# Edge attention on one core: scores taken four units at a time, with eight rows of relu kept instead of four

## The chip, the cores and the metric

The kernel runs on one core of one Trainium2 chip. The metric is the device time of one launch in microseconds (us), as the median of several runs. The engines are called PE (matmul), ACT (scalar), DVE (vector), POOL and SP (which issues the DMA transfers).

## The reference, cut to what matters

Four layers run over 128 graphs of 64 nodes with 256 features. The change lies in the second layer, an attention over 512 edges:

```python
x = x + _L0_gnn_ref(h, adj, ...)
h = jnp.maximum(_layernorm(x, axis=-1), 0.0)
Xq = (H @ W_lin.T).reshape(bt, n, h, dh)
Xv = (H @ W_val.T).reshape(bt, n, h, dh)
Qs = Xq[:, src]
Kt = Xq[:, dst]
e = jnp.einsum('behd,hd->beh', jax.nn.leaky_relu(Qs + Kt, LRELU_SLOPE), a)
e = e + jnp.log(A0[src, dst] + EPS)[None, :, None]
...
attn = ex / denom[src]
Y = jax.ops.segment_sum(attn[..., None] * Vt, src, num_segments=n)
return Y @ W_out.T
```

Here `e` is the score of an edge. The leaky relu is split into a linear part and a relu part; the relu part is what the text calls the scores.

## The kernel before

The second layer is the function `edge_attention`. It works in four quarters (`q` from 0 to 3) of 32 graphs. A quarter has four groups (`m`), a group has eight units (`i`), and a unit is one graph. Group 4 of a quarter (`m == NJ`) is at the same time group 0 of the next quarter. Everything is ordered by hand: each engine runs its own list of calls, and semaphores tie the lists together.

For each unit PE does `gather` (two matmuls into `c_pZ`, L1158), ACT does `relu` (two activations into one of the rows `relu_rows[i % RB]`, L1375), and PE later does `score` (L1173), which multiplies the rows of two units by a sign table into four strips of 32 partitions of `c_pE`. These matmuls have only 32 columns of weights; their form in the trace is 128\*32. The matmuls of `linear` (L1131) have the same form. All other matmuls around them have the form 128\*128.

While group `m` is scored, the rows of group `m + 1` are projected (`project`, L53 to L55, four calls in a group, after units 1, 3, 5 and 7; the text calls them projections 0 to 3), and the input of group `n = m + 2` is prepared:

- PE `turn_back` (L1109), then DVE `add_x` (L1453), `measure` (L1461) and `moments` (L1470, L1473), then POOL `normalise` (L1062, L1066, L1069) and DVE `normalise` (L1480), then PE `turn` (L1119), ACT `hi_halves`, DVE `lo_halves` (L1486), PE `linear` (L1131), ACT `copy_linear`, PE `turn_linear` (L1137), DVE `split_lin` (L1500).
- Each projection goes into the one bank `c_pU`. ACT `split_hi` (L1370) and DVE `split_lo` (L1509, L1512) empty it, and the next projection waits until `split_lo` is done.

DVE runs its own list strictly in order: `add_x`, `measure`, `split_lo` of projection 0, `moments`, `normalise`, `split_lo` of 1, `lo_halves`, `split_lo` of 2, `split_lin`, `split_lo` of 3. In group 4 the softmax over the scores is woven in (`softmax_step`, L1521 to L1527; it begins with L1521, which reads the finished `c_pE` after `add_linear`, L1179). After group 4 PE turns to the weighted sums of the quarter, beginning with `fill` (L1198). The tile `c_by_dst`, the attention matrix by destination, is written by ACT (L1418) and read by PE in that part alone. The last quarter has only groups 1 to 3, and nothing is prepared for `n` of 4 or more, so its group 2 has projections but no turns, and its group 3 has neither.

The relu rows are a ring of `RB = 4`, in the tile `c_relu`, which also serves as room for the full attention matrix after the scores. No semaphore protects the ring; the order of PE does (a `gather` stands behind the `score` that reads the row which this unit's relu will overwrite).

Of the kernel before, what the change touches and what calls it, by code (L numbers as in the profile page):

```python
# [12 lines left out]
P = 128  # L13
BATCH, NODES, D = 128, 64, 256
ROWS = BATCH * NODES
KD = D // P
# [4 lines left out]
EDGES = 512  # L21
# [46 lines left out]
def allocator(nc, ctx):  # L68
    def sb(name, shape, dt=F32):
        at = -(-nc.sbuf_base // 32) * 32  # L70
        gap = -at % LINE // 4
        if gap:
            ctx.enter_context(nc.sbuf_tensor(name + "_gap", [P, gap], F32))
        return ctx.enter_context(nc.sbuf_tensor(name, shape, dt))

    def ps(name, shape, dt=F32):
        return ctx.enter_context(nc.psum_tensor(name, shape, dt))

    return sb, ps
# [834 lines left out]
def edge_attention(core, x, x2, tables, h_rows, spilled, pairs, late):  # L914
# [4 lines left out]
    GG = GT * TILE_GRAPHS  # L919
    NJ = QT // GT  # L920
# [4 lines left out]
    with ExitStack() as ctx:  # L925
        sb, ps = allocator(nc, ctx)
        tab = tables.tab
        by_dst = sb("c_by_dst", [P, NODES, NODES])
# [6 lines left out]
        vals = sb("c_vals", [P, QT + AHEAD * GT, D])  # L935

        lin = sb("c_lin", [P, 2 * P])
        RB = 4
        dense_rows = sb("c_relu", [P, RB * KD * EDGES])
        relu_rows = [dense_rows[:, b * KD * EDGES:(b + 1) * KD * EDGES].rearrange("p (k c) -> p k c", k=KD) for b in range(RB)]  # L940

        def lin_cols(v, block):

# [46 lines left out]
        with nc.Block() as block:  # L990
# [109 lines left out]
            def _(pe):  # L1100
# [33 lines left out]
                def turn_linear(q, m):  # L1134
                    pe.wait_ge(sem["lin_row"], NJ * q + m + 1)
                    for t in range(GT):
                        last = nc.tensor.matmul(pT[:, 1, HEADS * t:HEADS * (t + 1)], lin_row[:, t * P:(t + 1) * P], tab["strip"][:, :],  # L1137
                                                start=True, stop=True)
                    last.then_inc(sem["lin_t"], 1)
# [12 lines left out]
                def gather(q, m, i):  # L1152

                    gi = QG * q + GG * m + i
                    pe.wait_ge(sem["s_lo"], QT * q + GT * m + i // 2 + 1)
                    for k in range(KD):
                        wait(pe, sem["r_done"], KD * (gi - 2) + k + 1)
                        nc.tensor.matmul(pZ[i % 2][:, k, :], keys[:, i, k * P:(k + 1) * P], tab["both"][:, :],  # L1158
                                         start=True, stop=True).then_inc(sem["z_mm"], 1)

                def score(q, m, u):

                    pair = (GG * m + 2 * u) % QG // 2
                    if pair == 0 and not m:
                        pe.wait_ge(sem["s_lo"], GT)
                    if pair == 0 and m:
                        pe.wait_ge(sem["soft"], SOFT * q + 1)
                    at = SLOTS - 2 - 2 * pair
                    for k in range(KD):
                        for i in (2 * u, 2 * u + 1):  # L1170
                            pe.wait_ge(sem["r_done"], KD * (QG * q + GG * m + i) + k + 1)
                            rows = SLOTS * (2 * (i % 2) + k)
                            nc.tensor.matmul(pE[rows:rows + SLOTS, :], tab["sign"][:, k, at:at + SLOTS],  # L1173
                                             relu_rows[i % RB][:, k, :], start=pair == 0, stop=False)

# [68 lines left out]
                def group(q, m, end=2 * NJ):  # L1244

                    n = m + 2
                    for i in range(GG):
                        gather(q, m, i)
                        if m == 0:
                            if i == 0:  # L1250
                                turn(q, 1)
                            if i == 1:
                                linear(q, 1)
                        elif n < end:
                            if i == 5:
                                turn(q, n)
                            if m == NJ and i == GG - 1:
                                turn_linear(q, n)
                                turn_attention(q)
                        if m + 1 < end and i % 2:  # L1260
                            project(q, m + 1, i // 2)
                        if i and i % 2 == 0:
                            score(q, m, i // 2 - 1)
                        elif i == 0 and m > 1:
                            score(q, m - 1, GG // 2 - 1)
                            if m == NJ:
                                add_linear(q)
                        if m == 0:
                            if i == 2:
                                turn_linear(q, 1)  # L1270
                            if i == 3:
                                turn_back(q, 2)
                            if i == GG - 1:
                                turn(q, 2)
                        elif n < end:
                            if i == 0:
                                turn_back(q, n)
                            if i == 6:
                                linear(q, n)
                            if m < NJ and i == GG - 1:  # L1280
                                turn_linear(q, n)

                def body(q, last=False):
                    top = NJ - 1 if last else NJ
                    for m in range(1, top + 1):
                        group(q, m, NJ if last else 2 * NJ)
                    score(q, top, GG // 2 - 1)
                    if last:
                        add_linear(q)
                        turn_attention(q)  # L1290
                    fill(q, 0)
                    fill(q, 1)
                    for n in range(2, NF):
                        fill(q, n)
                        turn_full(q, n - 2, last)
                    turn_full(q, NF - 2, last)
                    turn_full(q, NF - 1, last)
                    sums(q, 0)
                    for h in range(NH):
                        if h + 1 < NH:  # L1300
                            sums(q, h + 1)
                        project_out(q, h)
# [44 lines left out]
                pe.wait_ge(tables.rows, COLS_KEPT)  # L1347
                group(0, 0)
                linear(0, 2)
                score(0, 0, GG // 2 - 1)  # L1350
                turn_linear(0, 2)
                for q in range(NQ):
                    body(q, last=q == NQ - 1)

            @block.scalar
            def _(act):
# [15 lines left out]
                def relu(q, m, i):  # L1372
                    for k in range(KD):
                        act.wait_ge(sem["z_mm"], KD * (QG * q + GG * m + i) + k + 1)
                        nc.scalar.activation(relu_rows[i % RB][:, k, :], pZ[i % 2][:, k, :], ACT.Relu).then_inc(sem["r_done"], 1)  # L1375

# [69 lines left out]
            def _(dve):  # L1446
# [103 lines left out]
                def group(q, m, end=2 * NJ):  # L1550
                    n = m + 2
                    for i in range(GG):
                        if m == 0:
                            if i == 0:
                                lo_halves(q, 1)
                            if i == 2:
                                split_lin(q, 1)
                        elif n < end:
                            if i == 5:
                                lo_halves(q, n)  # L1560
                            if i == GG - 1:
                                split_lin(q, n)
                        if m == NJ and i == 0:
                            softmax_step(q, 0)
                        if m == NJ and i == GG - 1:
                            lo_of_attention(q)
                        if m and n < end and i == 3:
                            normalise(q, n)
                        if m + 1 < end and i % 2:
                            split_lo(q, m + 1, i // 2)  # L1570
                        if m == 0:
                            for at, part in ((3, add_x), (4, measure), (4, moments), (6, normalise), (7, lo_halves), (7, split_lin)):
                                if i == at:
                                    part(q, 2)
                        elif n < end:
                            for at, part in ((0, add_x), (0, measure), (1, moments)):
                                if i == at:
                                    part(q, n)
                        if m == NJ and i == 2:
                            softmax_step(q, 1)  # L1580
                        if m == NJ and i == 4:
                            softmax_step(q, 2)
                            softmax_step(q, 3)
# [926 lines left out]
```

## Time and profile before

| what | value |
|---|---|
| median of 3 runs | 2089.72 us (2087.96 to 2090.39) |
| the profiled execution, its own time | 2089.05 us |
| its span in the trace | 2087.5 us |
| PE busy | 1974.2 us, 95% of the span |
| DVE busy | 1252.9 us, 60% |
| ACT busy | 999.8 us, 48% |
| POOL busy | 223.9 us, 11% |
| edge attention in the span | from about 1143 us to about 1672 us |

The table is one execution. Times inside the span count from its start. Matmuls overlap each other, so lengths of work on PE are best read from start to start, and a busy PE is not yet a PE that never waits. A row of the timeline gives the start, the length, the engine, the line and the operation; a bracket at its end gives the idle time of the engine ahead of it and the instruction that ended it.

### The profile page before, as it was taken

What the parts mean: (1) busy time and instruction counts of PE and PEld (TensorE: products, weight loads), DVE (VectorE), ACT (ScalarE), POOL (GpSimd) and SP (SyncE); (2) the same over time, 40 slices, a digit from 0 to 9 for tenths busy, and PEclk for the clock granted to TensorE, in tenths of its full rate; (3) what the DMA queues carried; (4) which work ended last, traced back from release to release, by engine and by line L of the source; (5) the groups of instructions that cost most, each with busy time, mean ns of one, the idle gap of its engine ahead of it and who ended that gap; (6) DMA issues with size and microseconds to landing.
All of it is one profiled execution on the core that took longest, in us unless ns stands there. A gap on an engine that the chain in (4) does not pass through costs nothing. (4 is left out here: it accounts for less than half of the span.)

```text
span 2087.5 us, 33853 instructions
## 1 busy us (share of the span) xinstructions
PE 1974.2 (95%) x12438; PEld 1636.0 (78%) x12438; DVE 1252.9 (60%) x2627; ACT 999.8 (48%) x1675; POOL 223.9 (11%) x202
## 2 busy tenths in 40 slices
PE   6998999999999999999999799999999889897998
PEld 6997888888899999888887456657575778686997
DVE  7453665454455555654744666666664588886786
ACT  2553564433334433332322464563636246575996
POOL 1000000010110111011011350110100011100100
PEclk9999999999999999999999999999999989998999
DMA  3101001000100000100003221423213122001232
GB/s 117 61 21 41 0 0 41 0 0 0 40 1 0 0 0 0 31 1 41 40 0 117 95 71 51 143 81 113 98 43 125 50 80 64 22 0 51 81 101 91
DMA packets 81486, 99.92 MB, mean 48 GB/s; under 512 B 7408, under 2 KB 73584, under 8 KB 79088
## 3 DMA queue, kind: packets, MB, share of 16 engines
q1 hardware_dynamic: 81392, 98.65, 14.5%
q8 instruction: 61, 1.00, 0.2%
q14 instruction: 33, 0.27, 0.0%
HBM read 61.78 MB, written 33.55 MB: 46 GB/s over the span
## 5 line engine op out<-in xcount | busy, mean ns | idle before, releaser
L675 ACT ACTIVATE b_gate<-b_pG,b_bias 128x512 f32<-128x512 f32 (+1 forms) x504 | 304.2, 633 | 357.1 <-PE b_pG L55 356.4
L53 PE MATMUL b_pG<-b_xshi,b_whi 128*128 128x512 f32 (+1 forms) x1008 | 367.7, 365 | 6.6 <-DVE b_xslo L732 5.8
L55 PE MATMUL b_pG<-b_xshi,b_wlo 128*128 128x512 f32 (+1 forms) x1008 | 366.8, 364 | 0.0
L54 PE MATMUL b_pG<-b_xslo,b_whi 128*128 128x512 f32 (+1 forms) x1008 | 366.8, 364 | 0.0
L728 DVE CAST b_xshi<-HT 128x512 fp32r<-128x512 f32 (+3 forms) x144 | 59.6, 456 | 268.0 <-PE b_pG L55 267.7
L53 PEld LDWEIGHTS b_pG<-b_xshi,b_whi 128*128 128x128 f32 x1008 | 189.7, 188 | 33.9 <-DVE b_xslo L732 6.0
L54 PEld LDWEIGHTS b_pG<-b_xslo,b_whi 128*128 128x128 f32 x1008 | 189.8, 188 | 25.6
L55 PEld LDWEIGHTS b_pG<-b_xshi,b_wlo 128*128 128x128 f32 x1008 | 189.6, 188 | 25.8
L53 PE MATMUL b_pG<-b_hshi,b_whi 128*128 128x512 f32 (+1 forms) x576 | 205.1, 356 | 0.0
L54 PE MATMUL b_pG<-b_hslo,b_whi 128*128 128x512 f32 (+1 forms) x576 | 205.1, 356 | 0.0
L55 PE MATMUL b_pG<-b_hshi,b_wlo 128*128 128x512 f32 (+1 forms) x576 | 205.1, 356 | 0.0
L683 ACT ACTIVATE b_tc<-b_cell 128x512 f32<-128x512 f32 (+1 forms) x144 | 83.7, 581 | 213.4 <-DVE b_cell L871 111.6
L696 POOL TENSOR_TENSOR b_gate<-b_gate 128x512 f32<-128x512 f32 (+1 forms) x72 | 83.4, 1158 | 930.9 <-ACT b_gate L675 930.9
L1375 ACT ACTIVATE c_relu<-c_pZ 128x512 f32<-128x512 f32 x256 | 138.2, 596 | 35.7 <-PE c_pZ L1158 34.5
L53 PEld LDWEIGHTS b_pG<-b_hshi,b_whi 128*128 128x128 f32 x576 | 108.1, 188 | 12.5
L55 PEld LDWEIGHTS b_pG<-b_hshi,b_wlo 128*128 128x128 f32 x576 | 108.1, 188 | 12.5
L54 PEld LDWEIGHTS b_pG<-b_hslo,b_whi 128*128 128x128 f32 x576 | 108.1, 188 | 12.4
L732 DVE TENSOR_TENSOR b_xslo<-HT,b_xshi 128x512 fp32r<-128x512 f32 (+1 forms) x144 | 101.4, 746 | 2.5
L875 DVE TENSOR_TENSOR HT<-b_gate,b_tc 128x512 f32 (+3 forms) x72 | 51.9, 720 | 67.0 <-ACT b_tc L683 67.0
L1158 PE MATMUL c_pZ<-t_both,c_keys 128*128 128x512 f32 x256 | 87.8, 426 | 0.0
L1158 PEld LDWEIGHTS c_pZ<-t_both,c_keys 128*128 128x128 f32 x256 | 42.6, 191 | 45.3 <-issue 31.9
L878 DVE TENSOR_TENSOR b_tc<-b_gate,b_tc 128x512 f32<-128x512 f32 (+1 forms) x72 | 44.0, 611 | 54.7 <-ACT b_tc L683 54.7
(344 smaller groups left out, 3976.5 us busy)
## 6 DMA issues: line engine op xcount, KB each, us to landing
a_xt<-in_x SPq DMA_DIRECT2D x16, 512.0 KB, 5.5
h_scratch<-HT SPq DMA_DIRECT2D x4, 2048.0 KB, 7.6
l_x<-in_x SPq DMA_DIRECT2D x16, 512.0 KB, 3.9
l_w<-h_scratch SPq DMA_DIRECT2D x16, 512.0 KB, 5.0
x_scratch<-l_x SPq DMA_DIRECT2D x16, 512.0 KB, 3.1
c_x<-x_scratch SPq DMA_DIRECT2D x32, 256.0 KB, 3.7
x_scratch<-c_x SPq DMA_DIRECT2D x32, 256.0 KB, 2.5
l_x<-x_scratch SPq DMA_DIRECT2D x16, 512.0 KB, 3.8
```

The costliest lines, as they stand in the source:

```text
L53: nc.tensor.matmul(out, w_hi, x_hi, start=first, stop=False)
L54: nc.tensor.matmul(out, w_hi, x_lo, start=False, stop=False)
L55: return nc.tensor.matmul(out, w_lo, x_hi, start=False, stop=last)
L675: nc.scalar.activation(gate[s][:, g, 0:plan.n], pG[s][:, g, 0:plan.n], SIG[g], bias=bias[:, plan.p - 1, 2 * g + s:2 * g + s + 1])\
L683: nc.scalar.activation(tc[s][:, 0:plan.n], cell[b][:, s, 0:plan.n], ACT.Tanh).then_inc(tanh_ready, 1)
L696: nc.gpsimd.tensor_tensor(gate[s][:, I, 0:plan.n], gate[s][:, I, 0:plan.n], gate[s][:, G, 0:plan.n], ALU.mult).then_inc(ig_ready, 1)
L728: nc.vector.tensor_copy(plan.flat(xs_hi[b][:, k, :]), plan.windows(it, b, k, t))\
L732: last = nc.vector.tensor_tensor(plan.flat(xs_lo[b][:, k, :]), plan.windows(it, b, k, t), plan.flat(f32(xs_hi[b][:, k, :])), ALU.subtract)
L875: nc.vector.tensor_tensor(plan.windows(it, b, s, t), plan.flat(gate[s][:, O, :]), plan.flat(tc[s][:, :]), ALU.mult).then_inc(h_ready, 1)
L878: nc.vector.tensor_tensor(tc[s][:, 0:n], gate[s][:, O, 0:n], tc[s][:, 0:n], ALU.mult).then_inc(h_ready, 1)
L1158: nc.tensor.matmul(pZ[i % 2][:, k, :], keys[:, i, k * P:(k + 1) * P], tab["both"][:, :], start=True, stop=True).then_inc(sem["z_mm"], 1)
L1375: nc.scalar.activation(relu_rows[i % RB][:, k, :], pZ[i % 2][:, k, :], ACT.Relu).then_inc(sem["r_done"], 1)
```

## The change

The ring of relu rows grows from four to eight. The first four stay in `c_relu`, the other four lie in `c_by_dst`. `score` is called twice in a row, four units in one go: units 0 to 3 of a group after projection 2 of the same group's unit 5, and units 4 to 7 after projection 0 in the next group. The first softmax step moves from unit 0 to unit 2 of group 4, because `add_linear` moves from unit 0 to unit 1.

```diff
-        RB = 4
-        dense_rows = sb("c_relu", [P, RB * KD * EDGES])
-        relu_rows = [dense_rows[:, b * KD * EDGES:(b + 1) * KD * EDGES].rearrange("p (k c) -> p k c", k=KD) for b in range(RB)]
+        RB = GG
+        dense_rows = sb("c_relu", [P, RB // 2 * KD * EDGES])
+        halves_of_ring = (dense_rows[:, :], by_dst[:, :, :].rearrange("p i j -> p (i j)"))
+        relu_rows = [part[:, b * KD * EDGES:(b + 1) * KD * EDGES].rearrange("p (k c) -> p k c", k=KD)
+                     for part in halves_of_ring for b in range(RB // 2)]
...
-                        if i and i % 2 == 0:
-                            score(q, m, i // 2 - 1)
-                        elif i == 0 and m > 1:
-                            score(q, m - 1, GG // 2 - 1)
+                        if i == GG // 2 + 1:
+                            score(q, m, 0)
+                            score(q, m, 1)
+                        elif i == 1 and m > 1:
+                            score(q, m - 1, 2)
+                            score(q, m - 1, 3)
                             if m == NJ:
                                 add_linear(q)
...
-                    score(q, top, GG // 2 - 1)
+                    score(q, top, 2)
+                    score(q, top, 3)
...
-                score(0, 0, GG // 2 - 1)
+                score(0, 0, 2)
+                score(0, 0, 3)
...
-                        if m == NJ and i == 0:
+                        if m == NJ and i == 2:
                             softmax_step(q, 0)
```

In the changed file the lines of PE's list stand two further down (L1173 is L1175, L1131 is L1133) and those of DVE's list six further down (L1473 is L1479).

PE, a regular group, from the end of projection 2 to the gather of unit 7. `c_pU` is the bank of the projections, `c_pZ` that of the gathers, `c_pE` holds the scores, `c_pT` takes the linear part. Before:

```order
L55 MATMUL c_pU<-t_wqv_hi,c_hTlo 128x512
L1158 MATMUL c_pZ<-t_both,c_keys 128x512 x2
L1173 MATMUL c_pE<-c_relu,t_sign 32x512 x4
L1131 MATMUL c_pT<-c_hThi,t_wl 32x512 x2
L1131 MATMUL c_pT<-c_hTlo,t_wl 32x512 x2
L1158 MATMUL c_pZ<-t_both,c_keys 128x512 x2
```

The same place with the change:

```order
L55 MATMUL c_pU<-t_wqv_hi,c_hTlo 128x512
L1175 MATMUL c_pE<-c_relu,t_sign 32x512 x8
L1160 MATMUL c_pZ<-t_both,c_keys 128x512 x2
L1133 MATMUL c_pT<-c_hThi,t_wl 32x512 x2
L1133 MATMUL c_pT<-c_hTlo,t_wl 32x512 x2
L1160 MATMUL c_pZ<-t_both,c_keys 128x512 x2
```

Two scores (x8) now stand here where one (x4) did, and a gather separates them from the linear matmuls, which touched a score before. One such score less stands between projection 0 and projection 2 at each of the two places after units 2 and 4.

PE, the border between two regular groups, from turning the linear part to projection 0. Before:

```order
L1137 MATMUL c_pT<-t_strip,c_lin_row 128x4 x4
L1158 MATMUL c_pZ<-t_both,c_keys 128x512 x2
L1173 MATMUL c_pE<-c_relu,t_sign 32x512 x4
L1109 MATMUL c_pT<-t_ident,l_w_53 128x128 x8
L1158 MATMUL c_pZ<-t_both,c_keys 128x512 x2
L53 MATMUL c_pU<-t_wqv_hi,c_hThi 128x512
```

With the change:

```order
L1139 MATMUL c_pT<-t_strip,c_lin_row 128x4 x4
L1160 MATMUL c_pZ<-t_both,c_keys 128x512 x2
L1111 MATMUL c_pT<-t_ident,l_w_53 128x128 x8
L1160 MATMUL c_pZ<-t_both,c_keys 128x512 x2
L53 MATMUL c_pU<-t_wqv_hi,c_hThi 128x512
```

The score ahead of the turn back is gone from here; it follows, with another one, behind projection 0.

DVE, group 4 of the first quarter, from the end of group 3 to its normalise. `l_x_50` and `l_w_52` are the input tiles of the group being prepared. Before:

```order
L1512 TENSOR_TENSOR c_keys<-c_pU,c_keys 64x256 x2
L1521 TENSOR_TENSOR c_work<-c_pE,t_log_w 128x512
L1453 TENSOR_TENSOR l_x_50<-c_pT,l_x_50 128x1024
L1459 MEMSET c_ve 128x4
L1461 BN_STATS c_st<-l_x_50 128x6 x4
L1509 COPY c_vals<-c_pU 128x256
L1512 TENSOR_TENSOR c_keys<-c_pU,c_keys 64x256 x2
L1468 MEMSET c_unused 128x1
L1470 BN_AGGR c_mv<-c_st 128x2 x4
L1473 TENSOR_TENSOR c_ve<-c_ve,c_mv 128x4
L1523 SCALAR_TENSOR_TENSOR c_work<-t_cut,c_work 128x512
L1480 TENSOR_SCALAR l_w_52<-l_x_50,c_mv,c_rstd 128x256 x2
```

With the change:

```order
L1518 TENSOR_TENSOR c_keys<-c_pU,c_keys 64x256 x2
L1459 TENSOR_TENSOR l_x_50<-c_pT,l_x_50 128x1024
L1465 MEMSET c_ve 128x4
L1467 BN_STATS c_st<-l_x_50 128x6 x4
L1515 COPY c_vals<-c_pU 128x256
L1518 TENSOR_TENSOR c_keys<-c_pU,c_keys 64x256 x2
L1474 MEMSET c_unused 128x1
L1476 BN_AGGR c_mv<-c_st 128x2 x4
L1479 TENSOR_TENSOR c_ve<-c_ve,c_mv 128x4
L1527 TENSOR_TENSOR c_work<-c_pE,t_log_w 128x512
L1529 SCALAR_TENSOR_TENSOR c_work<-t_cut,c_work 128x512
L1486 TENSOR_SCALAR l_w_52<-l_x_50,c_mv,c_rstd 128x256 x2
```

The first softmax step (L1521, now L1527) moves from ahead of `add_x` to behind `moments`, next to the first scan (L1523, now L1529).

## Rows read from the trace of the kernel before

**Rows 1.** Windows: length, busy PE, PEld, DVE, ACT, POOL, PE clock, DMA, GB/s.

```profile
1194.00:1200.00 6.00, 3.74 (x20) 1.11 (x20) 1.43 (x2) 1.45 (x2) 6.00 (x3) 0.72 0.53 175
1346.24:1365.15 18.91, 18.23 (x108) 10.51 (x104) 11.99 (x30) 13.21 (x26) 3.09 (x3) 1.00 0.27 84
```

**Rows 2.** Timeline of PE, group 3 of the second quarter.

```profile
1365.15 1.09 PE L1109 MATMUL c_pT<-t_ident,l_w 128*128 128x128 f32 x8
...
1366.55 0.40 PE L53 MATMUL c_pU<-t_wqv_hi,c_hThi 128*128 128x512 f32 x1
...
1370.32 0.50 PE L53 MATMUL c_pU<-t_wqv_hi,c_hThi 128*128 128x512 f32 x1
...
1374.42 1.09 PE L1119 MATMUL c_pT<-t_ident,l_w 128*128 128x128 f32 x8 [0.33 <-DVE l_w L1480]
1375.74 0.50 PE L53 MATMUL c_pU<-t_wqv_hi,c_hThi 128*128 128x512 f32 x1 [0.23 <-DVE c_keys L1512]
...
1377.23 0.62 PE L1158 MATMUL c_pZ<-t_both,c_keys 128*128 128x512 f32 x2
1377.78 1.06 PE L1173 MATMUL c_pE<-c_relu,t_sign 128*32 128x512 f32 x8
1378.67 0.59 PE L1131 MATMUL c_pT<-c_hThi,t_wl 128*32 128x512 f32 x1
...
1379.64 0.74 PE L1158 MATMUL c_pZ<-t_both,c_keys 128*128 128x512 f32 x2
1380.22 0.40 PE L53 MATMUL c_pU<-t_wqv_hi,c_hThi 128*128 128x512 f32 x1
...
1381.61 0.95 PE L1137 MATMUL c_pT<-t_strip,c_lin_row 128*128 128x4 f32 x8
...
1383.07 1.06 PE L1173 MATMUL c_pE<-c_relu,t_sign 128*32 128x512 f32 x8
```

**Rows 3.** Timeline of DVE, the same group.

```profile
1366.28 1.23 DVE L1453 TENSOR_TENSOR l_x<-c_pT,l_x 128x1024 f32<-128x1024 f32 x1 [0.81 <-PE c_pT L1109]
...
1372.01 2.35 DVE L1480 TENSOR_SCALAR l_w<-l_x,c_mv,c_rstd 128x256 f32<-128x256 f32 x2 [1.12 <-POOL c_rstd L1062]
...
1382.60 0.36 DVE L1500 COPY c_lin<-c_pT 64x16 f32<-64x16 f32 x2 [3.06 <-PE c_pT L1137]
...
1383.43 0.86 DVE L1512 TENSOR_TENSOR c_keys<-c_pU,c_keys 64x256 fp32r<-64x256 f32 x2
```

**Rows 4.** Timeline of all engines, group 4 of the second quarter.

```profile
1390.62 1.22 DVE L1523 TENSOR_TENSOR_SCAN c_work<-t_cut,c_work 128x512 f32<-128x512 f32 x1
...
1390.78 1.86 POOL L1062 TENSOR_TENSOR c_rstd<-c_ve,c_mhalf 128x4 f32<-128x4 f32 x1 [16.57 <-DVE c_ve L1473]
...
1395.09 1.09 PE L1119 MATMUL c_pT<-t_ident,l_w 128*128 128x128 f32 x8 [1.18 <-DVE l_w L1480]
...
1396.41 0.50 PE L53 MATMUL c_pU<-t_wqv_hi,c_hThi 128*128 128x512 f32 x1 [0.23 <-DVE c_keys L1512]
```

**Rows 5.** Timeline of PE, end of group 4 and first matmul of `fill`.

```profile
1399.75 0.62 PE L1131 MATMUL c_pT<-c_hThi,t_wl 128*32 128x512 f32 x2 [0.23 <-DVE c_hTlo L1486]
...
1404.39 1.07 PE L1173 MATMUL c_pE<-c_relu,t_sign 128*32 128x512 f32 x8
1405.38 0.50 PE L1198 MATMUL c_pZ<-edge_pairs,c_attnhi 128*128 128x512 f32 x1
```

**Rows 6.** Timeline of the last quarter: projection 2 of group 1, then group 3.

```profile
1582.65 0.50 PE L53 MATMUL c_pU<-t_wqv_hi,c_hThi 128*128 128x512 f32 x1 [0.23 <-DVE c_keys L1512]
...
1604.53 0.61 PE L1158 MATMUL c_pZ<-t_both,c_keys 128*128 128x512 f32 x2
...
1614.54 1.08 ACT L1375 ACTIVATE c_relu<-c_pZ 128x512 f32<-128x512 f32 x2 [0.58 <-PE c_pZ L1158]
...
1616.65 1.13 PE L1179 MATMUL c_pE<-t_both,c_lin 128*128 128x512 f32 x2
```

**Rows 7.** Timeline of PE, the longest pause ahead of `linear` in the first quarter.

```profile
1196.26 1.07 PE L1131 MATMUL c_pT<-c_hThi,t_wl 128*32 128x512 f32 x2 [2.46 <-DVE c_hTlo L1486]
```

## The prediction

> **What bounds the kernel now.** I read the table of windows first [rows 1], then the timelines of PE and DVE for one regular group [rows 2, 3], then group 4 and the ends of the quarters [rows 4 to 6]. PE is busy for 18.23 of the 18.91 us of a regular group [rows 1], so the stage looks bound by PE. The rows of PE say otherwise. `turn` (L1119) waits for DVE's normalise, and projection 2 waits for DVE's `split_lo` (L1512) [rows 2]. A group is therefore a loop of two parts. From the turn back (1365.15) to projection 2 (1375.74) DVE's chain decides: 10.59 us, in which PE has slack. From projection 2 to the end of turning the linear part PE decides: it never waits, and 5.87 us pass until `turn_linear` (1375.74 to 1381.61) [rows 2]. What matters is thus in which part a score stands.
>
> DVE's chain in numbers: `add_x` starts at 1366.28, normalise at 1372.01 [rows 3], and projection 2 follows at 1375.74 [rows 2], 9.46 us after `add_x`. At the other end `split_lin` starts at 1382.60 and the last `split_lo` ends at 1383.43 + 0.86 = 1384.29 [rows 3], 2.68 us after `turn_linear`. Today the next turn back comes so late (another score is ahead of it) that `add_x` waits for it, 0.81 us in the row shown [rows 3].
>
> **The price of a score.** Two matmuls of 128\*128 form are 0.23 us apart: six take 1.39 (1380.22 to 1381.61) [rows 2]. A score that stands alone takes 0.99 us (1404.39 to 1405.38) [rows 5], one that is followed by `linear` 0.89, and `linear` behind it 0.97 [rows 2]. So joined pieces take 1.86 instead of 1.98. Two gathers take 0.46 by themselves, 0.55 ahead of a score (1377.23 to 1377.78), and 0.58 behind a burst of 32-column matmuls (1379.64 to 1380.22) [rows 2]. Each burst that vanishes thus saves 0.12 + 0.09 + 0.12 = 0.33 us of PE, and each score that stays costs 0.86 to 0.89.
>
> The change takes bursts away. By the order of PE's list a regular group had four (the last score of the group before, score 0, score 1, score 2 with `linear`) and now has three, since `linear` stands alone. Over the stage 19 vanish: four in each of three quarters, five in the last, two in the first group. That is 19 × 0.33 = 6.3 us of PE time.
>
> The Trainium skill has the rule behind this ("TensorEngine Tiling (Array Packing)", Key Properties): changing the tiling mode drains the TensorE. The trace agrees, with 0.33 us for a burst. By that rule alone, with PE as the bound, the kernel gains the 6.3 us; the rows of waits speak against it, and the case is the first rival below.
>
> **A regular group, term by term.** Projection 2 is followed by two scores: 1.49 + 0.09. The two scores take 1.86. The gather of unit 6 between two bursts takes 0.46 + 0.12 + 0.09 = 0.67. `linear` alone takes 0.99, the gather of unit 7 0.58, projection 3 1.39. Sum to `turn_linear`: 7.07 us, against 5.87. Then two routes lead to the next projection 2. Over the turn back: 1.46 less the 0.09 that a following score cost, so 1.37 (1381.61 to 1383.07) [rows 2], and the 10.59 of before: 19.03. Over DVE: 2.68 to the end of the last `split_lo`, 0.02, and 9.46 from `add_x`: 19.23. The longer decides: 19.23 against 18.91, **+0.32 us a group**. PE's part holds two scores as before, but both now stand ahead of `turn_linear`; before, one stood behind it, in the time in which DVE emptied projection 3. Leaving that space pays only until `add_x` meets the last `split_lo`. There are five such groups (the first quarter has one; between its projections 2 of groups 1 and 2 POOL's work on the edge pairs decides, so I add 0): **+1.6**.
>
> **Group 4.** From projection 2 of group 3 to that of group 4 pass 20.67 us (1375.74 [rows 2] to 1396.41 [rows 4]). With the change 7.07 + 2.70 us pass until `add_x`. From there it is the 9.46 of a regular group and what the softmax adds. Today POOL's power (L1062) starts at 1390.78 beside the scan (L1523) and takes 1.86 us [rows 4], while DVE's whole wait for it is 1.12 in a regular group [rows 3]; that adds 0.85, so 10.31. The change puts softmax step 0 between `moments` and the scan. At the least it fits in: step 0 and the scan end about when normalise starts today, −0.1. At the most the power again ends after the scan, which is now later by the length of step 0 (about 0.7): +0.6. No row shows the new pairing, so I take the middle, +0.25: 7.07 + 2.70 + 10.56 = 20.33, **−0.34**, three times: **−1.0** (bounds −2.1 and 0).
>
> The Trainium skill ("SBUF — State Buffer", SBUF: two separate sides) says that a DVE operation with two SBUF inputs and a GpSimd operation that reads SBUF exclude each other, the first to start holding the ports for its whole length. The row of 1.86 agrees. Step 0 reads one input from PSUM, so by this rule the power starts first, the scan waits for it and normalise comes 0.3 us later than today: the same as the middle.
>
> **The ends of the quarters.** From projection 2 of group 4 to `fill` pass 8.97 us (1396.41 [rows 4] to 1405.38 [rows 5]). In it stand score 2, `linear` and score 3; then four scores and `linear`. Two more scores are 1.72, one more burst 0.33. Today `linear` waits for `lo_halves` in between (0.23 us of idle PE in its row [rows 5], which I take as 0.41 with the restart, the 8.97 less the prices of its pieces); the longer way hides that. **+1.64** each, three times: **+4.9**. What follows `fill` starts from it and only shifts.
>
> **The last quarter.** From projection 2 of group 1 (1582.65) to the first gather of group 3 (1604.53) pass 21.88 us [rows 6]. Then: 7.07 to `turn_linear`, 2.73 until `split_lo` lets projection 0 go, and for group 2 1.58 + 1.86 + 0.58 + 0.46 = 4.48 (projection 0, two scores, two gathers), 3.77 (projection 0 to 1 through ACT and DVE, 1366.55 to 1370.32 [rows 2], now between projections 1 and 2), 4.48 and 1.39: 23.92, **+2.0**. Group 3 is bound by the loop of ACT and PE: ACT pauses 0.58 us ahead of every second relu [rows 6], since a gather stands behind a score that waits for a relu. With eight rows the gathers run ahead of the scores and two of four pauses go: 11.4 instead of 12.12 us (1604.53 to 1616.65) [rows 6], **−0.7** (bounds −1.4 and 0).
>
> **The start.** The first group wins 0.6 us ahead of its turn and then has one more score behind `linear`, in a stretch where the clock stands at 0.72 of full in the mean [rows 1]: 0.86 to 1.6. **+0.5**.
>
> **Costs of nothing.** Rows of relu written into `c_by_dst` instead of `c_relu` are the same activations; the tile is free then, and its next writer waits on PE work behind all scores. No DMA, no queue of SP or POOL is touched; loads are issued on `turn` and land a whole group ahead.
>
> **Sum:** 0.5 + 1.6 − 1.0 + 4.9 + 2.0 − 0.7 = +7.3 us. Against the profiled execution's own 2089.05 us that is 2096.4 us; it is 0.67 below the median of the runs, which I leave in the range.
>
> **Rivals.** (1) *PE's sum decides*, and the kernel is faster. It would be so if DVE's chain had slack. All 6.3 us would come back: 2082.8 us. The bracketed waits of L1119 and L53 [rows 2] speak against it. It decides only if the way from the turn back to projection 2 falls below PE's own sum there, about 8.9 us by the prices above, against 10.59. Chance 0.08. (2) *The overlap is better than I allow*: `add_x` follows the turn back directly (+0.1 instead of +0.32 a group, since 19.03 is the other route), the softmax fits in at its lower bound (−2.1), and group 3 saves 1.4. Sum 0.5 + 0.5 − 2.1 + 4.9 + 2.0 − 1.4 = +4.4; with the start at 0 as well it is +3.9, 2093.0 us, no change that can be told. Chance 0.2. (3) *The clock falls*. PE's pauses in the slack part grow, from 1.18 us ahead of `turn` in group 4 [rows 4] to some 1.5 us ahead of projection 1 in a group 1 (3.77 us of ACT and DVE against 2.3 of PE) and as much ahead of its `turn`. Behind a pause of 2.46 us [rows 7] the granted clock was at its lower level, 1.2 GHz, for part of the stretch, 0.72 in the mean over 6 us [rows 1], which is 1.7 us of PE lost. Two such stretches more give 2099.8 us. Chance 0.15. My forecast has the remaining 0.57.
>
> **The numbers.** A difference of 0.2%, 4.2 us, is about what a measurement of this kernel can tell from none. The forecast's own range is 2094.5 to 2098.5. The range that leaves out two in ten reaches from 2089.5, over rival 2, to 2100.0, over rival 3. Slower: 0.57 + 0.15 and a little of rival 2, 0.73. Same: 0.17. Faster: 0.10.
>
> **What the profile after would show.** Nineteen bursts less and less PE busy time, but longer idle ahead of `turn` and of projections 1 and 2. 19.2 us from turn back to turn back in a regular group; DVE without idle ahead of `add_x`; 10.6 us from projection 2 of group 4 to `fill`; L1062 in group 4 near 1.0 or near 1.9 us. The prediction fails if two scores in a row take clearly less than 1.86 us, or if projection 2 comes less than 9.4 us after `add_x`.

## The result, and the profile after

| | before | after |
|---|---|---|
| device time, median (lowest to highest) | 2089.11 us (2087.96 to 2090.39), 6 runs | 2097.19 us (2095.82 to 2101.83), 6 runs |
| ratio, 95% interval | 1 | 1.0039 (1.0027 to 1.0051) |
| profiled execution: own time, span | 2089.05, 2087.5 us | 2096.91, 2095.3 us |
| PE busy | 1974.2 us | 1966.9 us |
| first turn back of the stage to the last `fill` | 481.50 us | 490.05 us |

The change makes the kernel 8.1 us slower, though PE is busy for 7.3 us less in it (4.9 us less in a second trace of it, below). Forecast were 2096.4 us and 6.3 us less work. PE's list has 46 bursts of 32-column matmuls in the stage instead of 65: the 19 of the forecast. Line numbers move by 2 in PE's functions (turn back L1111, `turn` L1121, `linear` L1133, `turn_linear` L1139, gather L1160, score L1175, `add_linear` L1181, `fill` L1200) and by 6 or less in those of DVE and ACT (`add_x` L1459, normalise L1486, `split_lo` L1518).

The table of windows of the changed kernel, first: length, busy PE, PEld, DVE, ACT, POOL, granted clock, DMA share, GB/s. The first row is a regular group from turn back to turn back, the counterpart of the second row of [rows 1]. The other two are the same step, projection 2 to `turn_linear` of a group 1, in the last and in the second quarter.

```profile
1349.89:1369.18 19.29, 17.84 (x105) 10.64 (x105) 12.07 (x30) 13.10 (x27) 3.08 (x3) 1.00 0.25 82
1588.77:1597.38 8.61, 8.61 (x40) 4.16 (x41) 2.49 (x4) 4.25 (x8) 0.00 (x0) 0.80 0.74 263
1341.35:1348.39 7.04, 7.04 (x40) 3.53 (x41) 2.49 (x4) 4.25 (x8) 0.00 (x0) 1.00 0.49 157
```

A regular group takes 19.29 us instead of 18.91, though PE is busy for 0.39 us less of it. The second and third row do the same work at two clocks. At a mean of 0.80 of full, part of the stretch at the lower of the two levels (1.2 GHz), it takes 1.57 us more.

The timeline of PE in the changed kernel, group 3 of the second quarter, the group of [rows 2]:

```profile
1369.18 1.06 PE L1111 MATMUL c_pT<-t_ident,l_w 128*128 128x128 f32 x8
...
1372.04 1.92 PE L1175 MATMUL c_pE<-c_by_dst,t_sign 128*32 128x512 f32 x16
1373.89 1.20 PE L1160 MATMUL c_pZ<-t_both,c_keys 128*128 128x512 f32 x4
...
1378.52 1.09 PE L1121 MATMUL c_pT<-t_ident,l_w 128*128 128x128 f32 x8 [1.16 <-DVE l_w L1486]
1379.85 0.50 PE L53 MATMUL c_pU<-t_wqv_hi,c_hThi 128*128 128x512 f32 x1 [0.23 <-DVE c_keys L1518]
...
1381.45 1.92 PE L1175 MATMUL c_pE<-c_relu,t_sign 128*32 128x512 f32 x16
1383.30 0.73 PE L1160 MATMUL c_pZ<-t_both,c_keys 128*128 128x512 f32 x2
1383.96 0.62 PE L1133 MATMUL c_pT<-c_hThi,t_wl 128*32 128x512 f32 x2
...
1386.91 0.95 PE L1139 MATMUL c_pT<-t_strip,c_lin_row 128*128 128x4 f32 x8
1387.71 0.72 PE L1160 MATMUL c_pZ<-t_both,c_keys 128*128 128x512 f32 x2
1388.40 1.06 PE L1111 MATMUL c_pT<-t_ident,l_w 128*128 128x128 f32 x8
```

Each x16 row is two scores in a row. They take 1.85 us to the next row's start, less than twice the 0.99 of one that stands alone [rows 5]. The bracket of `turn` shows what became of the saving: PE waits 1.16 us for DVE's normalise, against 0.33 before [rows 2]. From projection 2 (1379.85) to `turn_linear` (1386.91) PE works without a wait, and needs 7.06 us. No score stands between `turn_linear` and the next turn back any more.

The timeline of DVE behind that `turn_linear`:

```profile
1387.89 0.36 DVE L1506 COPY c_lin<-c_pT 64x16 f32<-64x16 f32 x2 [4.23 <-PE c_pT L1139]
...
1388.72 0.86 DVE L1518 TENSOR_TENSOR c_keys<-c_pU,c_keys 64x256 fp32r<-64x256 f32 x2
1389.61 1.22 DVE L1459 TENSOR_TENSOR l_x<-c_pT,l_x 128x1024 f32<-128x1024 f32 x1
```

`split_lin` (L1506) waits for PE, for 4.23 us instead of 3.06 [rows 3]. `add_x` (L1459) has no bracket: it follows `split_lo` at once, where it had waited 0.81 us for the turn back [rows 3]. The way over DVE decides, as forecast.

Group 4 of the second quarter, all engines:

```profile
1394.24 0.69 DVE L1527 TENSOR_TENSOR c_work<-c_pE,t_log_w 128x512 f32<-128x512 f32 x1
1394.28 1.01 POOL L1064 TENSOR_TENSOR c_rstd<-c_ve,c_mhalf 128x4 f32<-128x4 f32 x1 [15.97 <-DVE c_ve L1479]
...
1394.97 1.23 DVE L1529 TENSOR_TENSOR_SCAN c_work<-t_cut,c_work 128x512 f32<-128x512 f32 x1
...
1395.37 1.66 POOL L1068 TENSOR_TENSOR l_w<-l_x,c_mv 128x512 f32<-128x512 f32 x1
...
1396.23 2.06 DVE L1486 TENSOR_SCALAR l_w<-l_x,c_mv,c_rstd 128x256 f32<-128x256 f32 x2
```

The power (L1064) starts beside softmax step 0 (L1527) and takes 1.01 us, not 1.86 as beside the scan [rows 4]. Now L1068, which starts beside the scan, is long: 1.66 us, where the operation takes 1.04 elsewhere (below).

The end of that group, PE:

```profile
1399.55 0.50 PE L53 MATMUL c_pU<-t_wqv_hi,c_hThi 128*128 128x512 f32 x1
...
1408.31 1.93 PE L1175 MATMUL c_pE<-c_by_dst,t_sign 128*32 128x512 f32 x16
1410.16 0.50 PE L1200 MATMUL c_pZ<-edge_pairs,c_attnhi 128*128 128x512 f32 x1
```

1399.55 to 1410.16 is 10.61 us, against 8.97 before.

The last quarter, PE, as in [rows 6]:

```profile
1588.77 0.50 PE L53 MATMUL c_pU<-t_wqv_hi,c_hThi 128*128 128x512 f32 x1 [0.23 <-DVE c_keys L1518]
...
1608.30 0.50 PE L53 MATMUL c_pU<-t_wqv_hi,c_hThi 128*128 128x512 f32 x1 [1.29 <-DVE c_keys L1518]
...
1614.15 1.07 PE L1160 MATMUL c_pZ<-t_both,c_keys 128*128 128x512 f32 x4
...
1625.58 0.70 PE L1181 MATMUL c_pE<-t_both,c_lin 128*128 128x512 f32 x1
```

In group 2 the two scores of group 1's second half now stand between projections 0 and 1, and PE then waits 1.29 us ahead of projection 2 for DVE (the row of 1608.30). From 1588.77 to the gathers of group 3 at 1614.15 pass 25.38 us instead of 21.88, and 11.43 instead of 12.12 from there to `add_linear`.

### The profile page after: what moved, and what is told of

The parts are those of the page before. It is cut to its first block and busy times, and to the rows that moved or that the text cites. A ratio compares the mean times of both kernels' runs of the same rounds, so it can differ in the third digit from the quotient of the medians.

```text
span 2095.3 us, 33852 instructions
## 1 busy us (share of the span) xinstructions
PE 1966.9 (94%) x12438; PEld 1639.2 (78%) x12438; DVE 1250.9 (60%) x2627; ACT 996.2 (48%) x1675; POOL 222.9 (11%) x202
## 5 line engine op out<-in xcount | busy, mean ns | idle before, releaser
L1381 ACT ACTIVATE c_relu<-c_pZ 128x512 f32<-128x512 f32 x128 | 67.6, 600 | 38.5 <-PE c_pZ L1160 38.4
L1160 PE MATMUL c_pZ<-t_both,c_keys 128*128 128x512 f32 x256 | 82.7, 426 | 0.1
L1381 ACT ACTIVATE c_by_dst<-c_pZ 128x512 f32<-128x512 f32 x128 | 67.5, 602 | 22.4 <-PE c_pZ L1160 22.0
```

## The experiments

Theory: the cost lies in where the scores stand. From projection 2 to `turn_linear` every microsecond of PE is one of the kernel's. Behind the turn back and up to projection 2, PE has slack. Rivals: the ring of eight rows, with half of it in another tile, costs something by itself; or PE's work costs the same wherever it stands; or the clock does it.

The ratios below are those on record; they are not the quotient of the two medians, and can differ from it by 0.05%.

### The ring alone

The kernel before, with the scores in their old places.

```diff
-        RB = 4
-        dense_rows = sb("c_relu", [P, RB * KD * EDGES])
+        RB = GG
+        dense_rows = sb("c_relu", [P, RB // 2 * KD * EDGES])
+        halves_of_ring = (dense_rows[:, :], by_dst[:, :, :].rearrange("p i j -> p (i j)"))
```

> The kernel before with the ring of eight relu rows (four of them in the attention matrix's room) and every score where it was. The theory that the places of the scores cost the time: no change, within 1 us of the kernel before, since no instruction moves. The rival that the rows in the attention matrix's tile or the longer ring cost something: up to the whole +8 us of the change.

Measured: 2090.03 us (10 runs) against 2089.48 (22 runs), ratio 0.9998 (0.9988 to 1.0008). A regular group takes 18.91 us and the stage 481.59, as before (481.50). The eight rows cost nothing that can be told.

### Eight spare transposes in the slack part

The kernel before, with 8 transposes (0.97 us of PE) that nothing reads, behind the gather of unit 4 in thirteen groups.

```diff
+                        if m and n < end and i == 4:
+                            spare(q, n)
```

> The kernel before with eight spare transposes of a constant on PE behind the gather of unit 4, in 13 groups, in the part between turn back and projection 2 (their result is not used). Eight transposes take 0.8 us. Theory: PE has 1.4 us of waits in that part, so no change, at most +1 us. The rival that PE's sum of work decides the time of the stage: 13 x 0.8 = +10.5 us.

Measured: 2088.93 us (10 runs) against 2089.48, ratio 0.9997 (0.9988 to 1.0007). PE in the second quarter:

```profile
1374.19 1.03 PE L1248 MATMUL c_pT<-t_ident 128*128 128x128 f32 x8
1375.16 1.06 PE L1173 MATMUL c_pE<-c_relu,t_sign 128*32 128x512 f32 x8
...
1376.72 1.04 PE L1119 MATMUL c_pT<-t_ident,l_w 128*128 128x128 f32 x8
1377.65 0.50 PE L53 MATMUL c_pU<-t_wqv_hi,c_hThi 128*128 128x512 f32 x1
```

The brackets of `turn` and of projection 2 are gone: the transposes fill both waits. The brackets understate these: from `turn` to projection 2 pass 0.93 us here and 1.32 before [rows 2]. The loop keeps its length (18.90 us). Thirteen times 0.97 us of PE's work cost nothing here.

### The same transposes ahead of the turn back

The kernel before, in the same thirteen groups.

```diff
+                    if m > 2:
+                        for t in range(GT):
+                            for k in range(KD):
+                                nc.tensor.transpose(pTr[:, t, k * P:(k + 1) * P], tab["ident"][:, :], tab["ident"][:, :])
```

> The kernel before with the same eight spare transposes in the same 13 groups, but directly ahead of the turn back, in the part in which PE does not wait. Theory: every one counts but in the one group that POOL decides: 12 x 0.8 = +9.8 us. The rival that there is slack all around the loop: clearly less, under +5 us. (The rival of PE's sum gives +10.5 us here and in the run with the transposes behind unit 4 alike.)

Measured: 2098.78 us (5 runs) against 2089.48, ratio 1.0042 (1.0028 to 1.0056). PE:

```profile
1370.73 1.09 PE L1110 MATMUL c_pT<-t_ident 128*128 128x128 f32 x8
1371.66 1.04 PE L1113 MATMUL c_pT<-t_ident,l_w 128*128 128x128 f32 x8
...
1380.87 1.09 PE L1123 MATMUL c_pT<-t_ident,l_w 128*128 128x128 f32 x8 [0.32 <-DVE l_w L1484]
1382.19 0.50 PE L53 MATMUL c_pU<-t_wqv_hi,c_hThi 128*128 128x512 f32 x1 [0.23 <-DVE c_keys L1516]
```

The waits behind stand as before, and the regular group takes 19.77 us, 0.86 more; the stage is 10.75 us longer. The work is of the same kind as in the kernel above and costs 9.3 us in all. The place decides, not PE's sum.

### `linear` alone, a score behind it

The kernel before, with score 2 behind the gather of unit 7. As many scores as before stand on either side of `turn_linear`, but `linear` is no longer joined to one, so a group has one burst more.

```diff
+                        if i == GG - 1:
+                            score(q, m, 2)
                         if m + 1 < end and i % 2:
                             project(q, m + 1, i // 2)
-                        if i and i % 2 == 0:
+                        if i in (2, 4):
                             score(q, m, i // 2 - 1)
```

> The kernel before with linear ahead of score 2: linear behind the gather of unit 6, score 2 behind that of unit 7. No work is added, one burst of 32-column matmuls more in each group, in the part in which PE does not wait. Theory (0.33 us for a burst, and linear now waits some 0.1 us for lo_halves in a regular group and longer in group 4): +0.45 us a regular group, about +1.0 us at the end of each of three quarters, together about +7 us: 2096.5 us. The rival that a burst costs nothing of its own: +0.1 us a regular group and +3 us together.

Measured: 2096.15 us (6 runs) against 2089.38 (10 runs), ratio 1.0032 (1.002 to 1.0045). PE, and DVE's `lo_halves`:

```profile
1378.70 0.50 PE L53 MATMUL c_pU<-t_wqv_hi,c_hThi 128*128 128x512 f32 x1 [0.23 <-DVE c_keys L1514]
...
1379.56 1.23 DVE L1488 SCALAR_TENSOR_TENSOR c_hTlo<-c_pT,c_hThi 128x1024 fp32r<-128x1024 f32 x1 [0.92 <-ACT c_hThi L1361]
...
1380.19 0.62 PE L1158 MATMUL c_pZ<-t_both,c_keys 128*128 128x512 f32 x2
1380.93 0.62 PE L1131 MATMUL c_pT<-c_hThi,t_wl 128*32 128x512 f32 x2
...
1381.93 0.73 PE L1158 MATMUL c_pZ<-t_both,c_keys 128*128 128x512 f32 x2
1382.59 1.07 PE L1173 MATMUL c_pE<-c_relu,t_sign 128*32 128x512 f32 x8
...
1385.09 0.95 PE L1137 MATMUL c_pT<-t_strip,c_lin_row 128*128 128x4 f32 x8
```

From projection 2 to `turn_linear` 6.39 us pass instead of 5.87, and the regular group takes 19.42 instead of 18.91: +0.52 and +0.51. What PE loses in the part where it decides, the loop loses, and 6.8 us in all. The loss is more than the 0.33 us at which I price a burst. The difference is ahead of `linear`: the gathers take 0.74 us until it starts (1380.19 to 1380.93), and took 0.55 ahead of a score [rows 2]. These 0.19 us are a wait for `lo_halves` (L1488), though it has no bracket: that ends at 1379.56 + 1.23 = 1380.79, and `linear` starts 0.14 us later. Where a bracket names this wait, `linear` follows as closely (0.15 us in the kernel before, where `lo_halves` ends at 1399.60 [rows 5]). So the 0.52 us are 0.33 for the burst, as priced, and 0.19 of wait.

### The first scan behind normalise

The kernel before. It tells whether the long power of group 4 is the scan's doing.

```diff
+                        if m == NJ and i == 3:
+                            softmax_step(q, 1)
...
-                        if m == NJ and i == 2:
-                            softmax_step(q, 1)
```

> The kernel before with the first scan of the softmax behind DVE's normalise in group 4, so that POOL's power runs with no scan beside it. Theory: the power takes 1.0 us instead of 1.86, and projection 2 of group 4 comes about 0.9 us earlier behind that of group 3 (19.8 instead of 20.67 us); lo_halves comes a scan later, so the way from there to fill gets about 1.1 us longer (10.1 instead of 8.97), and the whole is unchanged within 1 us. The rival that the power is long for another reason (its input lands late): 1.86 us again.

Measured, one run: 2092.5 us. Group 4, all engines:

```profile
1391.32 1.01 POOL L1062 TENSOR_TENSOR c_rstd<-c_ve,c_mhalf 128x4 f32<-128x4 f32 x1 [16.55 <-DVE c_ve L1473]
...
1392.37 2.35 DVE L1480 TENSOR_SCALAR l_w<-l_x,c_mv,c_rstd 128x256 f32<-128x256 f32 x2 [1.12 <-POOL c_rstd L1062]
1392.41 1.04 POOL L1066 TENSOR_TENSOR l_w<-l_x,c_mv 128x512 f32<-128x512 f32 x1
```

Without a scan beside it the power takes 1.01 us, and the way between the projections 2 of groups 3 and 4 is 19.80 us instead of 20.67. The scan then delays what comes later (projection 2 to `fill` 10.23 instead of 8.97), so the stage is 1.04 us longer. The whole time is 3.1 us above the kernel before, of one run, so 2 us of it are not the stage's.

### Both scores ahead of `turn`

The changed kernel, with scores 0 and 1 behind the gather of unit 5 and ahead of `turn`.

```diff
                         gather(q, m, i)
+                        if i == GG // 2 + 1:
+                            score(q, m, 0)
+                            score(q, m, 1)
...
-                        if i == GG // 2 + 1:
-                            score(q, m, 0)
-                            score(q, m, 1)
-                        elif i == 1 and m > 1:
+                        if i == 1 and m > 1:
```

> The changed kernel with one move: scores 0 and 1 stand right behind the gather of unit 5, ahead of the turn and of projection 2, so in the part in which PE waits for DVE. Theory of the places: from projection 2 to turn_linear 7.07 us fall to about 5.4 (then bound by the emptying of projection 2), the part before it becomes bound by PE at about 11 us, and a regular group takes about 17.6 us instead of 19.2 (18.9 before). A quarter gains about 3.7 us against the kernel before, the sum is about -9.7 us: 2079 us. The rival that pairs of scores, or the mode of 32 columns in long bursts, cost time wherever they stand: 2097 us as the change. The rival that DVE's chain cannot be shortened because the last split_lo is what ends it: no better than 2089 us.

Measured: 2083.18 us (6 runs) against 2089.48, ratio 0.9967 (0.9955 to 0.998), faster than both kernels. PE:

```profile
1359.31 0.62 PE L1133 MATMUL c_pT<-c_hThi,t_wl 128*32 128x512 f32 x2 [0.62 <-DVE c_hTlo L1492]
...
1371.96 1.93 PE L1175 MATMUL c_pE<-c_relu,t_sign 128*32 128x512 f32 x16
1373.81 1.09 PE L1121 MATMUL c_pT<-t_ident,l_w 128*128 128x128 f32 x8
1374.66 0.48 PE L53 MATMUL c_pU<-t_wqv_hi,c_hThi 128*128 128x512 f32 x1
```

The waits ahead of `turn` and projection 2 are gone, and a regular group takes 17.78 or 18.06 us. It is not the 17.6 I expected, and the kernel is 4 us slower than the 2079 expected. A new wait stands ahead of `linear`: PE arrives before DVE's `lo_halves` and loses 0.62 us. Projection 2 to `fill` takes 11.82 us in the first quarter, against 9.33 in the others. In part it is a stretch of low clock at 1278.9, which the kernel before does not have. The other part came before that stretch:

```profile
1273.40 1.28 ACT L1385 ACT_TABLE_LOAD   x1
...
1277.65 1.05 PE L1139 MATMUL c_pT<-t_strip,c_lin_row 128*128 128x4 f32 x8 [0.99 <-ACT c_lin_row L1369]
```

ACT loads a table here, 1.28 us long, ahead of its work for the first quarter's softmax; in the second quarter there is no load at this place, and no such wait. `copy_linear` is late by it, and projection 2 to `turn_linear` takes 5.57 us instead of 4.62. The 1.54 us that remain lie in the low stretch.

### One score ahead of `turn`, one behind the gather of unit 6

The changed kernel again, with one of the two scores moved behind it, to fill that new wait.

```diff
                         gather(q, m, i)
+                        if i == GG // 2 + 1:
+                            score(q, m, 0)
...
-                        if i == GG // 2 + 1:
-                            score(q, m, 0)
+                        if i == GG // 2 + 2:
                             score(q, m, 1)
-                        elif i == 1 and m > 1:
+                        if i == 1 and m > 1:
```

> The changed kernel with score 0 ahead of the turn and score 1 behind the gather of unit 6, joined to linear. As many bursts and as much work as with both ahead of the turn (2083 us, 17.8 to 18.1 us a regular group). Theory: from projection 2 to turn_linear 5.8 us, then DVE's route of 2.7 + 9.46: 17.9 us a regular group, 2083 us again, now bound by DVE on one side. The rival that only the number of scores ahead of the turn decides: half way between the change and both ahead, 2090 us.

Measured: 2081.98 us (5 runs) against 2089.38, ratio 0.9962 (0.9948 to 0.9976). PE:

```profile
1372.87 1.09 PE L1121 MATMUL c_pT<-t_ident,l_w 128*128 128x128 f32 x8 [0.15 <-DVE l_w L1487]
1374.20 0.50 PE L53 MATMUL c_pU<-t_wqv_hi,c_hThi 128*128 128x512 f32 x1 [0.23 <-DVE c_keys L1519]
```

A regular group takes 18.03 or 18.12 us. The wait ahead of `linear` is gone in the regular groups, the small ones ahead of `turn` and projection 2 are back. The kernel isn't measurably better than with both scores ahead (the intervals overlap), and it beats the kernel before by 7.4 us.

### The change once more

One more profile of the changed kernel, for the stretches of low clock.

> The changed kernel once more, for a second trace. If the clock falls behind the longer pauses of the change, its two extra stretches at the lower level (at 1312.7 and 1589.1 us) come again at the same steps of the program; if they depend on where the stage happens to start, they move, go or others come. Regular groups 19.2 to 19.3 us and group 4 19.7 us in any case.

Measured, one run: 2095.91 us. Regular groups of 19.22 and 19.29 us and a group 4 of 19.72 us repeat. The low clock does not. The first trace has two stretches that the kernel before lacks: one at 1312.7, in the part behind `fill`, and one at 1589.1, behind projection 2 of the last quarter's group 1. This one has neither. It has two others, at 1214.1 and 1463.3, both behind projection 2 of a group 1, and lacks one that the kernel before and the first trace have at 1233.4 and 1234.2. The one at 1214.1 costs nothing in all: from projection 2 of the first quarter's group 1, in which it lies, to that of group 2 pass 21.30 us, as in the other two traces, since POOL's work decides there. So this trace has one stretch that costs (1463.3) where the kernel before has one (1233.4), and their stages can be compared as they are. The window of the step with the stretch at 1463.3, in the third quarter:

```profile
1462.90:1471.50 8.60, 8.60 (x40) 4.16 (x41) 2.49 (x4) 4.24 (x8) 0.00 (x0) 0.80 0.48 160
```

The step that took 7.04 us in the second quarter of the first trace takes 8.60 here, at a clock of 0.80.

### The pauses of groups 1 filled

The changed kernel, with the 8 spare transposes behind the gathers of units 3 and 4 of each group 1, where the change leaves PE idle longest.

```diff
+                        if m == 1 and i in (3, 4):
+                            spare(q, n)
```

> The changed kernel with eight spare transposes of a constant on PE behind each of the gathers of units 3 and 4, in group 1 of each quarter alone, where the change leaves PE its longest pauses (about 1.4 us ahead of projection 1 and 1.5 us ahead of the turn). Theory: the clock falls behind these pauses in some of the groups 1; filled, they cost nothing (the part from turn back to projection 2 stays 10.5 us) and no group 1 has a stretch at the lower level: 1.5 us less for each one that goes, 2095 us in the mean. The rival that the clock falls for another reason (the phase of the stage, the DMA traffic beside group 1): stretches there again, 2097 us.

Measured: 2097.33 us (9 runs) against 2090.01 (12 runs), ratio 1.0034 (1.0024 to 1.0044). The window from turn back to projection 2 of the second quarter's group 1:

```profile
1332.94:1343.47 10.53, 9.21 (x55) 7.36 (x54) 8.39 (x21) 7.99 (x17) 3.08 (x3) 1.00 0.83 242
```

It stays 10.53 us long with the spare work in it, as expected. None of this trace's four groups 1 has a stretch of low clock; the change's two traces have one and two of four, that of before none. But the one in the part behind `fill` is there again, at 1314.9, and the time is that of the change (2095 us were expected, but the intervals are too wide to tell a stretch of 1.5 us for certain). So the pauses of groups 1 aren't shown to cause the stretches, nor cleared: the traces are too few.

## Why the prediction was right

It forecast 2096.4 us and slower, and 2097.19 was measured. By its own steps, with the same places of both traces:

| step | forecast | measured |
|---|---|---|
| start, first turn back to that of group 1 | +0.5 | +0.71 (57.51 to 58.22) |
| five regular groups | +1.6 | +1.61 |
| group 4, three times | −1.0 | −2.85 |
| projection 2 of group 4 to `fill`, three times | +4.9 | +4.90 |
| last quarter to the gathers of group 3 | +2.0 | +3.50, of it 1.54 low clock |
| its group 3 | −0.7 | −0.69 |
| low clock behind the first `fill` | 0 (rival 3) | +1.45 |
| ahead of the stage, and behind it | 0 | +0.37, −1.05 |

The rows add up to +7.95, the spans differ by 7.87. The stage alone is 8.55 longer by its two ends, and its rows add up to 8.63. The last row lies in parts that the change does not touch; it moves from trace to trace (+1.30 ahead and +0.07 behind in the second).

**The two routes.** Forecast were 7.07 us to `turn_linear` and 19.23 us a regular group over DVE. The trace has 7.06 and 19.21 to 19.29. The absent wait of `add_x` names the route. The spare transposes test the two parts of the loop: nothing in the slack part, 0.86 us a group ahead of the turn back. The way to `turn_linear` is 1.19 us longer than before, which is a second score at 0.86 and a burst at 0.33. Rival 1, that PE's sum decides, fell: PE's busy time shrank by 5 to 7 us and the kernel got slower. Bursts taken away make the kernel faster only where the scores stand in the slack part: with both ahead of `turn` it is 6.3 us faster than before, with one of them 7.4.

**The Trainium skill** says that changing the tiling mode drains the TensorE ("TensorEngine Tiling (Array Packing)", Key Properties). The trace agrees: joined, two scores take 1.85 us and not 1.98, and one burst more cost 0.33 us in its experiment, beside 0.19 us of wait. The rule says nothing of where that price is paid, and here that decides the sign.

**Group 4, the step that was mis-sized.** The mechanism was right: the group gets shorter, because step 0 moves into a gap and no score stands behind `turn_linear`. The size was −0.95 a group, not −0.34, and beyond my lower bound (−0.7). The term was `add_x` to projection 2: forecast 10.56, measured 9.94 (1389.61 to 1399.55). I had taken the middle of two pairings. It was the lower one: power beside step 0, and normalise 6.62 us behind `add_x` (1389.61 to 1396.23), as before. The bound then missed that normalise itself gets shorter, 2.06 us where it took 2.28 in this group and 2.35 in a regular one [rows 3]. That the scan is what stretches the power is shown by the kernel with the scan behind normalise: 1.01 us and −0.87 us a group.

What sets the length of normalise can be read from the traces, though no run was made for it. It has two halves on DVE, and two operations of POOL run beside them. At the start of the stage in the changed kernel POOL is ahead of DVE, and the second half has no POOL operation beside it:

```profile
1151.80 1.10 POOL L1071 TENSOR_TENSOR l_w<-l_w,c_rstd 128x512 f32<-128x512 f32 x1
1152.04 1.33 DVE L1486 TENSOR_SCALAR l_w<-l_x,c_mv,c_rstd 128x256 f32<-128x256 f32 x2
```

That half takes 0.40 us. Each half that has a POOL operation beside it ends 0.15 to 0.16 us behind that operation, in every trace of this case. Here it is the first half, at 1153.05 behind 1152.90. The median length of a half is 1.20 us. In group 4 of the changed kernel L1068 has started beside the scan and ends only 0.80 us behind the start of normalise, not 1.01 as before, so the first half is 0.95 us long and not 1.16. Of the 0.37 us between the 10.31 us of the group before and the 9.94 after, this is 0.22; 0.03 is an earlier start and 0.12 an earlier `split_lo` behind it. So POOL's share of normalise lengthens the very chain of DVE that decides in the slack part. Whether the kernel would gain by moving that share, no run tests.

The Trainium skill ("SBUF — State Buffer", SBUF: two separate sides) gives the ports to whichever of the two operations starts first, for its whole length. By this rule the scan had to wait for the power; it started at 1394.97, while the power by its row (spans on POOL are rough) ran until 1394.28 + 1.01 = 1395.29, and was 1.23 us long as ever. The other half of the rule fits: the POOL operation that starts beside the scan is held. The normalise 0.3 us later, which the prediction took from that rule, did not come.

**The clock, rival 3 in part.** Two stretches of low clock, which cost 1.45 and 1.54 us, lie in the changed kernel's stage and not in that of before. One is where rival 3 put it, behind the pauses of a group 1; the other is not. The second trace has neither. Without them the stage would be 8.55 − 1.45 − 1.54 = 5.56 us longer, and in the second trace it is 487.00, 5.50 longer, with as many costly stretches as the kernel before. So my sum of +7.3 was 1.7 too high by group 4, and the clock, which the sum had at nothing, made up for it. That the total came so close is luck; that the kernel got slower, and by which steps, is not. The medians differ by 8.1 us, 2.6 more than these 5.5. The runs without a trace may hold such stretches too, but no row shows them. What makes the clock fall in the one execution and not in the next stays open.

## What to carry to other kernels

Before work is moved to save PE time, divide the loop at the places where PE waits. Work added ahead of a wait for another engine is free as long as it fits into the wait. Work added between the end of PE's last wait and the row that another engine waits for costs nearly its full length. The same 0.97 us of PE was worth nothing in one place and 0.86 us in the other, and a change that takes bursts away gained 7 us or lost 8 by where it put the ones it kept. Where two changes of the clock are as large as the terms of a sum, compare step by step before believing a total that fits.

## What the runs showed of the hardware

- A scan of DVE isn't held by a small operation of POOL (the power, 128x4) that runs already: it started 0.32 us before the power's end in the row above, and took 1.23 us. But a POOL operation that starts beside a scan ends 0.80 to 0.84 us behind the scan's end, in every trace that has such a pair: the power at 1390.78 + 1.86 = 1392.64 with the scan until 1391.84 [rows 4], L1068 at 1397.03 with the scan until 1396.20. In a regular group they take 1.01 and 1.04 us, nearly the same, so it isn't shown whether a longer operation would end as soon. Spans on POOL are rough, but normalise, which waits for the power, starts at 1392.75 and confirms the first.
- A half of DVE's normalise (128x256) takes 0.40 us with no operation of POOL beside it, and otherwise ends 0.15 to 0.16 us behind the POOL operation beside it, which makes it up to 1.24 us long.
- Stretches of low clock that cost about 1.5 us each came and went between two profiled executions of the changed kernel. The first has them at 1312.7 and 1589.1, the second at 1214.1 and 1463.3, and the one at 1234.2 in the first is missing from the second.
